# A gated recurrence and a routed mixture of experts on one core: the shared expert of all four batches ahead of the block loop

## The reference

```python
x = x + attn(layernorm(x))
xf = layernorm(x).reshape(2048, 256)
w, idx = gate(xf)                       # 6 of 32 experts for each token
c = zeros(2048, 32).at[token, idx].add(w)
g, u = xf @ w11[e].T, xf @ w33[e].T     # every routed expert, 128 wide
y = sum over e of ((silu(g) * u) * c[:, e]) @ w22[e].T
shared = (silu(xf @ sw1.T) * (xf @ sw3.T)) @ sw2.T     # 256 wide
out = x + y + shared
```

## Time and profile before

| | us |
|---|---|
| median of three runs | 528.32 |
| the profiled execution | 528.58 |
| its span | 526.8 |
| outside the span | 1.78 |
| TensorE busy | 366.7 |
| VectorE busy | 302.6 |
| GpSimd busy | 266.6 |
| ScalarE busy | 189.4 |

### The profile page before, as it was taken

The page is one execution under the profiler, slowest core; times in us unless marked ns, Lnnn a source line. Parts: engine busy times, 40 slices in busy tenths (PEclk is TensorE's granted clock), DMA queues, the critical chain, the costliest instruction groups (busy, mean ns, idle before and its releaser), DMA issues.

```text
span 526.8 us, 8882 instructions
## 1 busy us (share of the span) xinstructions
PE 366.7 (70%) x1662; PEld 274.2 (52%) x1663; DVE 302.6 (57%) x868; ACT 189.4 (36%) x502; POOL 266.6 (51%) x261
## 2 busy tenths in 40 slices
PE   2944725347264164747499999999999999998810
PEld 1421414233253044234388888888888888874400
DVE  4759849946688833312155555555555555553798
ACT  2587371024433002000155455444555445540000
POOL 3401000578378877773055555555555555562561
PEclk9986875588585585779699999999999999998965
DMA  8400000131121359999465555555555555406992
GB/s 265 188 0 1 1 0 0 56 132 63 62 103 71 112 194 435 392 384 347 140 173 175 170 165 164 163 162 169 167 170 163 172 158 171 118 8 237 420 384 73
DMA packets 42495, 86.00 MB, mean 163 GB/s; under 512 B 8165, under 2 KB 33517, under 8 KB 42096
## 3 DMA queue, kind: packets, MB, share of 16 engines
q1 hardware_dynamic: 26848, 52.73, 29.5%
q0 software_dynamic: 10752, 28.34, 14.9%
q10 hardware_dynamic: 4880, 4.76, 2.7%
HBM read 49.97 MB, written 40.01 MB: 171 GB/s over the span
## 4 chain that ended last, share of the span: by engine, by line
PE 55%; DVE 25%; ACT 8%; SPq 6%; issue 4%; DMA 3%; DVEq 0%; ACTq 0%
PE PS L1025 21%; PE PS L1039 11%; PE PS L1018 6%; PE PS L946 5%; SPq L263 3%; PE PS L1032 3%; PE PS L989 3%; PE PS L908 2%; SPq L264 2%; DVE expert_weights L280 2%; DMA bucket_rows<-pad_rows 1%; PE PS L917 1%; DVE st L580 1%; PE PS L936 1%; DVE resid L285 1%
## 5 line engine op out<-in xcount | busy, mean ns | idle before, releaser
L388 POOL DMA_INDIRECT choice_rows<-block_out_s,block_meta x128 | 125.9, 984 | 107.3 <-issue 67.4
L373 POOL DMA_INDIRECT bucket_rows<-payload,dest x96 | 111.0, 1156 | 86.8 <-DVE dest L749 58.2
L1025 PE MATMUL PS<-expert_weights,block_rows_t 128*128 x512 | 133.3, 383 | 0.0
L1025 PEld LDWEIGHTS PS<-expert_weights,block_rows_t 128*128 128x128 f32 x512 | 88.5, 193 | 6.9
L1039 PE MATMUL PS<-expert_weights,block_hidden_t 128*128 x256 | 78.0, 386 | 0.0
L846 DVE SCALAR_TENSOR_TENSOR block_hidden_s<-block_silu_s,block_meta,PS 128x128 f32<-128x128 f32 x128 | 44.4, 347 | 45.6 <-ACT block_silu_s L528 43.3
L538 ACT ACTIVATE block_rows_t<-PS 128x256 f32<-128x256 f32 x128 | 49.0, 383 | 56.5 <-PE PS L1018 55.7
L528 ACT ACTIVATE block_silu_s<-PS 128x128 f32<-128x128 f32 x128 | 35.5, 277 | 63.7 <-PE PS L1025 63.7
L840 DVE COPY block_meta<-block_rows_s 128x2 f32 x128 | 23.1, 181 | 61.1 <-issue 61.1
L852 DVE COPY block_out_s<-PS 128x256 f32<-128x256 f32 x128 | 53.6, 418 | 4.1 <-PE PS L1039 4.0
L1018 PE MATMUL PS<-ident,block_rows_s 128*128 128x128 f32 x256 | 49.7, 276 | 8.1 <-DMA block_rows_s<-bucket_rows 7.7
(11 more groups left out here) (172 smaller groups left out, 463.0 us busy)
## 6 DMA issues: line engine op xcount, KB each, us to landing
block_rows_s<-bucket_rows SPq DMA_DIRECT2D x128, 160.0 KB, 2.2
expert_weights<-choice_rows SPq DMA_DIRECT2D x16, 768.0 KB, 14.7
expert_weights<-in_experts SPq DMA_DIRECT2D x1, 10368.0 KB, 31.8
bucket_rows<-pad_rows SPq DMA_DIRECT2D x21, 160.0 KB
resid<-in_x SPq DMA_DIRECT2D x4, 512.0 KB, 9.3
choice_rows<-block_out_s,block_meta POOLq DMA_INDIRECT x128
out<-resid ACTq DMA_DIRECT2D x16, 128.0 KB, 3.7
expert_weights<-in_experts SPq DMA_DIRECT2D x1, 1920.0 KB, 14.9
```

The source lines that it names most:

```text
L373: nc.gpsimd.indirect_dma_start(out=bucket_ap[:, :], out_offset=bass.IndirectOffsetOnAxis(ap=dest[:, b, t, k:k + 1], axis=0), in_=PAY[:, b ...
L388: nc.gpsimd.indirect_dma_start(out=choice_ap[:, :], out_offset=bass.IndirectOffsetOnAxis(ap=meta_id[:, slot, 1:2], axis=0), in_=yy[:, slot ...
L1025: ins = mm(PS[:, 2 + r, 0:2 * P], xT[:, r, k * P:(k + 1) * P], W[:, bass.ds(w + k * 2 * P, 2 * P)], start=(k == 0), stop=(k == KD - 1))
```

## The change

One constant is changed. The shared expert of all four batches runs ahead of the block loop, and the lists behind the loop (lines 562 and 1071, and the two conditions on `late` at line 879 on) are empty. The TensorE enters the block loop behind `shared_out` of batch 3.

```diff
-    SHARED_BEFORE = B // 2
+    SHARED_BEFORE = B
```

## The result

The changed kernel takes 545.75 us (median of four runs, 544.62 to 546.39) against 528.1 us before (with a fourth run beside the three above): ratio 1.0332, 95% interval 1.031 to 1.0354. It is 17.65 us slower; forecast were 543.0 us and a range of 540.5 to 546.0. The profiled execution took 546.39 us, its span is 544.6.

The account below looks back on a forecast made before the run. Each stage has its own limit: padding DMA and first row load ahead, TensorE in the loop, VectorE sums behind. 528.58 + 19.5 - 1.3 + 1.1 - 4.6 = 543.3, 543.0 us as median; range 540.5 to 546.0.

Parts of the forecast that it names:

- Front: Ahead of the loop: two more serial batches, 26 us less 6.4 of slack, start the loop at 276.73, +19.5 us.
- The clock: Two new TensorE gaps ahead of the loop: a clock fall costs 1.69 us, one in three, +1.1 us.
- The start of the loop: First transpose to fourth block's gate and up: warm start takes 5.9 us instead of 7.23, -1.3 us.
- the bound I gave: Start of the loop: largest gain thought possible, -2.3 us, three steps and nothing else.
- The loop: Block loop: 1.63 us a step as now, so no change in its length.
- The tail: Behind the loop: the VectorE's sums lose shared steps and end at 519.9 instead of 524.57, -4.6 us.
- The fourth meeting with the GpSimd: Tail: with the idle stretch gone, GpSimd tile 6 also runs beside VectorE adds and slows them, +2.94 us.
- Ahead of the change: Before the moved batches: the prediction had no term here, so no change.
- The first two rivals: Tail: sums bound by loads, 537.5 us, 6%; or earlier stores delay tiles, 0 to 1 back, 547 us, 8%.
- the third: Ahead of the loop: clock falls in both new gaps, 545.3 us, or 546.6 with a cold loop start, 14%.
- the one in which the front is bound by the TensorE itself: Ahead of the loop: next gate and up fills each gap, front only 3.0 us later, kernel faster at 525.4, 2%.

Follow-up runs that it names:

- e4: Changed kernel with two matmuls of 512 columns added in the gap between up and down of batches 1, 2 and 3; ratio 1.0477 to the kernel before.
- e10: The kernel of e4 run again in a later set; ratio 1.0397 to the kernel before.
- e3: Changed kernel with the shared expert of batches 2 and 3 run a second time behind the loop; ratio 1.0584 to the kernel before.
- e11: Changed kernel with six matmuls of one column added ahead of the loop, moving only the loop's place in the TensorE's program; ratio 1.0399 to the kernel before.
- e5: Kernel before with 32 one-column matmuls and their waits added on the TensorE ahead of the loop; ratio 1.0012.
- e2: Kernel before with the shared expert of batches 2 and 3 left out; ratio 0.9958.
- e12: The kernel of e2 run again in a later set; ratio 0.9916 to the kernel before.
- set 2: Second set of experiments, kernel before at 527.6 us: e5, e7, e8, and e8 with three batches ahead and one behind (ratio 0.9959).
- e7: Changed kernel with the shared expert pipelined by one batch, next gate and up ahead of this batch's down; ratio 1.0151 to the kernel before.
- e8: The kernel of e7 with the ScalarE's twelve padding issues split, three ahead of each batch's Silu; ratio 1.0011 to the kernel before.

## Why the prediction was right, and by how much each step was off

The direction, the mechanism and the range held, the range by 0.25 us only, and that is in part luck: two terms of 1.6 us each were put at nothing, and only the 0.9 us that the start of the loop gave beyond its forecast kept the time inside. By its steps, on the two profiled executions (their difference is 17.8 us):

- **Front, forecast +19.5.** From batch 1's gate and up (238.02) to the loop's start (280.05) are 42.03 us; less the 1.69 of the clock that is 40.34, and forecast were 276.73 - 236.43 = 40.30. The slack of 6.4 us was the only cover, and the release moved from the DMA to the last add as forecast.
- **The clock, forecast +1.1.** It was +1.69: one fall, of two possible. The odds of one in three were too low. In all profiles taken with unfilled gaps of 2.37 us (the two at the start and seven of the experiments), it fell in 9 of 17 such gaps ahead of the loop, and in none of the 6 that e4 and e10 filled. So the idle gap is shown to be the cause. Which gap it hits is not random in these profiles: ahead of the loop the gap next behind a fall never had one (5 of 5), the gap next behind one without a fall always had (3 of 3), so that of the two new gaps exactly one was hit in all three kernels with four serial batches and unfilled gaps (the changed one, e3, e11). No run shows why, and behind the loop it isn't so: e5 has two falls one after the other there.
- **The start of the loop, forecast -1.3.** It was -2.2: from the first transpose to the fourth block's gate and up about 5.0 us instead of 7.23, close to the bound I gave. In the profile after the first gate and up are 1.2 us apart (281.05, 282.23, 283.42) and only the next follows 1.63 behind (285.05), which is where the down matmuls begin; I had charged 1.63 for each.
- **The loop, forecast 0.** It was +1.6, the term that I did not have. I took the loop as unchanged because no instruction in it is changed; it stands 32 matmuls later in the TensorE's program, and its jump back costs up to 0.2 us more a turn, 0.11 in the mean of 14. e5 shows the dear jump in the kernel before and e11 the cheap one in the changed kernel. Why a place is dear no run here shows.
- **The tail, forecast -4.6.** It was -4.4 in the profile, -4.7 in e2's and -4.9 in e12's; e3 put it back in full. The fourth meeting with the GpSimd cost the 2.94 us forecast. The loads were no bound, as forecast.
- **Ahead of the change, forecast 0.** In the profile after, the last bucket rows are known at 212.75 instead of 211.61 on the VectorE, and batch 1's gate and up is 1.59 us later. This one and the four of set 2 lie at 212.6 to 213.1, with the same code up to there. One of the four is e5, the kernel before with a filler on the TensorE behind this point, and it lies at 213.05; that speaks for the one profile of the kernel before being an early one and against an effect of the change. Why the executions differ is open.

The sum of the misses is +0.6 - 0.9 + 1.6 + 0.2 + 1.6 = 3.1, which is 546.4 - 543.3.

The first two rivals did not come: the VectorE waited for no load but the first, and the earlier stores cost the tail no more than the 0.2 us by which it missed. Nor did the third, for the clock fell once. Of the rest, the one in which the front is bound by the TensorE itself is real but needs another program: with the batches pipelined the loop starts 8.6 us earlier (e7, 271.5 for 280.05; the two differ in falls of the clock too), and with the ScalarE's padding issues, which hold the first Silu, spread it starts 9.0 us earlier again (e8, 262.5). Even then all four batches ahead only reach the time of the kernel before. Three fit under the cover, and give 2.2 us.

## What to carry to other kernels

Work moved from behind a bound to ahead of it costs all that exceeds the slack there, and gives back only what stood on the chain that ends last: here 26 us for a slack of 6.4, against 4.4. Price the two ends separately, and look in the tail for what the moved work was hiding (here a GpSimd tile that ran while the VectorE waited). Before moving work into a stage, make it dense there: with the gaps filled by the next batch and the padding issues spread, the same stage took three batches under the same cover.

## What I had not expected of the hardware

- The step over the TensorE's jump back took 1.91, 1.92 and 2.07 us in turn with the loop at one place of the program and 2.09 at another; all other steps together took 181.9 us at both.
- Idle gaps of 2.37 us between dense groups of matmuls cost a fall of the clock in 9 of 17 cases ahead of the loop, 1.7 us each; filled down to 0.65 us, in none of 6.
- Between two sets on one chip the kernel before went from 527.6 to 559 us. In the disturbed profiles the twelve padding issues on the ScalarE's queue took 34 to 35 us instead of 15, and the loop 218 to 229 us instead of 209; the tail, which is the VectorE's, stayed within 0.5 us of that of the like kernel.
